# Cross-attention and FFN block on one core: x turned by VectorE in 32x32 pieces, its norm folded into q's, Wq loaded by row blocks

## What is computed

```python
x = x + xattn(layernorm(x), ctx, Wq, Wk, Wv, Wo, gq, bq, gk, bk)   # x: (2, 2048, 512), ctx: (2, 128, 512)
x = x + ffn(layernorm(x), Win, bin_, W1, b1, W2, b2, Wout, bout)

def xattn(h, ctx, ...):          # 16 heads of 32
    q, k, v = h @ Wq, ctx @ Wk, ctx @ Wv
    q, k = layernorm over the 32 of each head (q, gq, bq), (k, gk, bk)
    attn = softmax(q k^T / sqrt(32))
    return (attn v) @ Wo

def ffn(h, ...):
    s = h @ Win + bin_                                      # 64 columns
    g = (relu(s[..., None] * W1 + b1) * W2).sum(-1) + b2    # 16 units for each
    return g @ Wout + bout
```

## Time and profile before

| | |
|---|---|
| median of 3 runs | 443.71 us (442.64 to 443.96) |
| the profiled execution | 445.51 us, of which the span is 443.7 us |
| TensorE (PE) busy | 95% |
| VectorE (DVE) busy | 74% |
| ScalarE (ACT) busy | 71% |
| GpSimd (POOL) busy | 55% |
| packets on the DMA queue of SP, share of 16 engines | 50.5% |

### The profile page before, as it was taken

The page is one execution under the profiler, slowest core; times in us unless marked ns, Lnnn a source line. Parts: engine busy times, 40 slices in busy tenths (PEclk is TensorE's granted clock), DMA queues, the critical chain, the costliest instruction groups (busy, mean ns, idle before and its releaser), DMA issues.

```text
span 443.7 us, 7794 instructions
## 1 busy us (share of the span) xinstructions
PE 423.3 (95%) x2344; PEld 287.2 (65%) x2344; DVE 327.1 (74%) x652; ACT 315.3 (71%) x611; POOL 241.9 (55%) x326
## 2 busy tenths in 40 slices
PE   4999999999889999999999999999999999998994
PEld 2477887476557767576676757685665476556772
DVE  4888787746565999569874898479678985777765
ACT  5549768887487963899369974899559937953640
POOL 4419976586475484548156646165659036307084
PEclk9999999999999999999999999999999999999998
DMA  8662593965923339633493275705851980044005
GB/s 274 177 203 102 125 210 115 208 142 141 235 66 69 95 115 216 153 94 73 142 233 77 77 142 191 144 3 119 215 143 27 209 244 3 1 136 149 1 2 190
DMA packets 28106, 58.34 MB, mean 131 GB/s; under 512 B 8865, under 2 KB 9377, under 8 KB 24993
## 3 DMA queue, kind: packets, MB, share of 16 engines
q1 hardware_dynamic: 28064, 57.85, 50.5%
HBM read 22.18 MB, written 8.39 MB: 69 GB/s over the span
## 4 chain that ended last, share of the span: by engine, by line
PE 75%; DMA 7%; SPq 6%; POOL 3%; issue 3%; DVE 3%; ACT 1%; POOLq 1%; DVEq 0%; ACTq 0%
PE bank L2613 31%; PE bank L2619 9%; PE bank L2702 6%; PE bank L2690 6%; PE bank L2676 6%; PE bank L2705 4%; PE bank L2633 4%; PE bank L2755 3%; DMA out_dram<-x 3%; SPq L486 2%; SPq L433 2%; PE bank L2779 2%; DMA xin<-in_x_dram 2%; PE bank L2766 2%; DMA att<-in_L_xattn_Wk_dram 2%
## 5 line engine op out<-in xcount | busy, mean ns | idle before, releaser
L1074 DVE TENSOR_REDUCE mx<-bank 128x4 fp32r<-128x512 f32 x128 | 82.1, 684 | 21.9 <-PE bank L2676 21.5
L1854 ACT ACTIVATE prob<-bank 128x512 f32<-128x512 f32 x128 | 71.0, 609 | 16.6 <-PE bank L2690 10.7
L2702 PE MATMUL bank<-prob,v_kv 128*32 128x512 f32 x256 | 62.1, 599 | 0.0
L2705 PE MATMUL bank<-prob,den_sel 128*32 128x512 f32 x256 | 61.3, 599 | 0.0
L1935 ACT ACTIVATE hid<-s_in,b_col,w_col 128x256 f32<-128x256 f32 x105 | 56.8, 623 | 0.6 <-DVE s_in L1135 0.6
L2613 PE MATMUL bank<-wq_hi,zt_hi 128*128 128x512 f32 x128 | 51.5, 403 | 0.9 <-issue 0.9
L725 POOL TENSOR_TENSOR squares<-u 128x512 f32<-128x512 f32 x32 | 33.0, 1041 | 35.5 <-DVE ssq L1067 19.1
L737 POOL TENSOR_TENSOR qt_lo<-u,qt_hi 128x512 fp32r<-128x512 f32 x32 | 40.8, 1290 | 19.9 <-ACT qt_hi L1839 17.4
L2613 PE MATMUL bank<-wq_hi,zt_lo 128*128 128x512 f32 x128 | 50.6, 395 | 0.0
L2613 PE MATMUL bank<-wq_lo,zt_hi 128*128 128x512 f32 x128 | 50.6, 395 | 0.0
L1177 DVE SCALAR_TENSOR_TENSOR bank<-hid,w_col,bank 128x256 f32<-128x256 f32 x90 | 43.8, 487 | 5.1 <-ACT hid L1935 2.9
(11 more groups left out here) (175 smaller groups left out, 899.1 us busy)
## 6 DMA issues: line engine op xcount, KB each, us to landing
q_stack<-qt_hi SPq DMA_DIRECT2D x64, 256.0 KB, 4.7
...
```

The source lines that it names most:

```text
L1074: dve.tensor_reduce(mx[:, :].rearrange("p (g i j) -> p g i j", g=G, i=HC)[:, :, 2 * half + r, j], maxs_banks[T][half][j][r][:, :].rearrang ...
L1854: act.activation(prob[:, h % PR, :], score_bank[t][h][:, :], ACT.Exp, scale=SCALE).then_inc(exp_done, 1)
L2702: pe.matmul(at_bank[t][c][rows(n), :], v_kv[kv_of(t)][:, n * HD:(n + 1) * HD], prob[:, n % PR, :], start=True, stop=True)
L2705: ins = pe.matmul(den_bank[t][rows(n + 2), :], den_sel[:, c, :], prob[:, n % PR, :], start=c == 0, stop=c == C - 1)
```

## The change

**x.** It is loaded raw. load_x(T, half) brings two tiles with four DMAs of 32 partitions: partition group g gets columns 128 g to 128 g + 127 of x in pieces of 32 rows, so that a 32x32 transpose within partition groups (turn_x, VectorE, in place in xin) gives the turned tile. turn_z1 and z1_norm are gone, and z1_high reads xin. z1_low is done by VectorE for blocks 0 to 2 (z1_low_early) and by GpSimd from block 3 on. Since the rows that Wq meets are then in another order, Wq is loaded by four DMAs of 32 partitions in that order.

**The first norm.** Scaling a row of x by rstd scales q by it, and q is normed by head afterwards; so only the variance is needed, as an addition to q's sum of squares (add_eps: ssq + 32 eps var). The mean falls out if the columns of Wq sum to zero over the 512 inputs: sum_wq (TensorE, 4 fp32 matmuls of 128x512 against inv_d) and flatten_wq (VectorE, 4 of 128x512) take it out. The variance comes from a second load of each tile in its plain layout, xs (load_stats, 256 KB, 2 slots, stats1). guess1 and newton1 are gone.

**The start.** Wk comes in four loads, Wq ahead of x, and TensorE does 5 fp32 matmuls of 128x128 (spin) ahead of turn_ctx and 2 ahead of project_keys. wout_in and ctx_t move to other buffers; bout_row is loaded later.

All the written orders and bank tables are new. The core of the diff:

```diff
-            sp.dma_start(wk_in[:, :, :], Wk.rearrange("(c p) n -> p c n", p=P)).then_inc(wk_loaded, 16)
-            for j in range(TB):
-                sp.dma_start(xin[:, j, :], x_t[0, j]).then_inc(x_loaded[j], 16)
             for c in range(C):
-                sp.dma_start(wq_in[:, c, :], Wq[c * P:(c + 1) * P, :]).then_inc(wq_loaded[c], 16)
+                sp.dma_start(wk_in[:, c, :], Wk[c * P:(c + 1) * P, :]).then_inc(wk_loaded[c], 16)
+            wq_rows = Wq.rearrange("(q c e) n -> q e c n", q=G, c=C)
+            for g in range(G):
+                sp.dma_start(wq_in[HD * g:HD * (g + 1), :, :], wq_rows[g]).then_inc(wq_loaded[g], 16)
+            for half in range(2):
+                for g in range(G):
+                    sp.dma_start(x_parts[g][:, 2 * G * half:2 * G * (half + 1), :],
+                                 x_by_part[0, g][:, 2 * G * half:2 * G * (half + 1), :]).then_inc(x_loaded[g][half], 16)
...
-            def load_x(T, j):
+            def load_x(T, half):
 
-                sp.wait_ge(z1_turned, T * TB + j + 1 - TB)
-                sp.dma_start(xin[:, j, :], x_t[T, j]).then_inc(x_loaded[j], 16)
+                sp.wait_ge(zt_lo_done, T * TB - HT * (1 - half))
+                rows = slice(2 * G * half, 2 * G * (half + 1))
+                for g in range(G):
+                    sp.dma_start(x_parts[g][:, rows, :], x_by_part[T, g][:, rows, :]).then_inc(x_loaded[g][half], 16)
+
+            def load_stats(T, j):
+
+                if T * TB + j >= 2:
+                    sp.wait_ge(bn1_done, T * TB + j - 1)
+                sp.dma_start(xs[:, j % 2, :], x_t[T, j]).then_inc(xs_loaded[j], 16)
...
+            def z1_low(T, j):
+
+                if T == EARLY and j == 0:
+                    pool.wait_ge(zt_lo_done, EARLY * TB)
+                pool.wait_ge(zt_hi_done, T * TB + j + 1)
+                pool.tensor_tensor(zt_lo[:, j % 2, :, :].rearrange("p c (a s) -> p c a s", a=G), x_turned_of(j),
+                                   zt_hi[:, j % 2, :, :].rearrange("p c (a s) -> p c a s", a=G).bitcast(F32),
+                                   ALU.subtract).then_inc(zt_lo_done, 1)
...
+            def add_eps(T):
+
+                dve.wait_ge(mv1_done, T * TB + TB)
+                dve.wait_ge(ssq_done, T * TB + TB)
+                dve.scalar_tensor_tensor(out=ssq[:, :, :], in0=mv1[:, :, 1].unsqueeze(2).broadcast_to([P, TB, H]),
+                                         scalar=HD * EPS, in1=ssq[:, :, :], op0=ALU.mult, op1=ALU.add).then_inc(eps_added, 1)
+
+            def turn_x(T, j):
+
+                for g in range(G):
+                    dve.wait_ge(x_loaded[g][j // HT], T * 16 + 16)
+                dve.transpose(xin[:, j, :], xin[:, j, :]).then_inc(x_turned, 1)
...
+            def flatten_wq(c):
+
+                dve.wait_ge(wq_summed, 1)
+                dve.tensor_tensor(wq_in[:, c, :], wq_in[:, c, :], wq_mean_bank[:, :], ALU.subtract).then_inc(wq_flat, 1)
...
-            def z1_norm(T, j):
-                act.wait_ge(ln1_step, T * 7 + 7)
-                act.activation(xin[:, j, :], xin[:, j, :], ACT.Identity, bias=shift1[:, j:j + 1],
-                               scale=ln1[:, 3, j:j + 1]).then_inc(z1_done, 1)
...
+            def spin(dst, count):
+
+                for n in range(count):
+                    pe.matmul(dst[:, 0:P], inv_d[:, :], inv_d[:, :], start=True, stop=True)
...
-            def turn_z1(T, j):
-                pe.wait_ge(z1_done, T * TB + j + 1)
-                turn(z1_bank[T][j], columns(xin[:, j, :]), z1_turned)
+            def sum_wq():
+
+                pe.wait_ge(eyes, NEYES)
+                for c in range(C):
+                    pe.wait_ge(wq_centred, c + 1)
+                    ins = pe.matmul(wq_mean_bank[:, :], inv_d[:, :], wq_in[:, c, :], start=c == 0, stop=c == C - 1)
+                ins.then_inc(wq_summed, 1)
```

More of the change, by code:

```diff
@@ L27 @@
 LATE = 2
+EARLY = 3
 SUMMED = range(4, HH)
@@ L390, in _ @@
         def _(sp):
+            x_parts = [xin[HD * g:HD * (g + 1), :, :].rearrange("p j (a e) -> p (j a) e", e=P) for g in range(G)]
             column = lambda a: a.rearrange("(p o) -> p o", o=1)
@@ L437, in load_wout @@
             def load_wout():
-                for part in range(2):
-                    sp.wait_ge(kv_projected[part], NB)
+                sp.wait_ge(kv_projected[0], NB)
                 for half in range(2):
```

2636 lines of the change are left out of this document (1298 added, 1338 removed), and 32 rows, old and new, of tables (maxs_rows, score_bank).

## The result

The change made the kernel slower: 450.96 us median of 4 runs (449.72 to 452.18) against 443.83 of the kernel before (442.64 to 445.93), a ratio of 1.0157 with a 95% interval of 1.0113 to 1.0201. I had forecast 440.0. On another chip the changed kernel came out at 449.74 against 444.32, ratio 1.0136 (1.0097 to 1.0174).

A forecast was written before the change was run, and what follows sets the result against it. SP's loads at the start were taken as the bound: scores(0, 0) 6.0 us later, less 8.7 for turns and 0.9 for max_scores, gives -3.6, rounded to -3.7, from 443.7 to 440.0 us; range 430 to 447.

The forecast's parts named there:

- 9.6 us of TensorE's work behind scores(0, 0): After scores(0, 0), TensorE saves 8.7 us from 80 fewer turns and 0.9 us from two fewer pairs of max_scores.
- the bound of 1.4: VectorE's transpose of 128x512: upper bound of 1.4 us, from 8 times 0.17; 0.61 us was taken.
- the estimate of 1.24: VectorE's transposes for one tile: four of 128x128 at the Trainium skill's 311 ns, an estimated 1.24 us.
- the size of the start, +6.0: At the start, scores(0, 0) can't begin before 81.8 us, against 75.8 before: 6.0 us later, set by SP's loads.
- Nothing of this waits long: SP's loads up to stack_max(0) hardly wait: stack_q needs qt_lo, expected at about 55 us, before SP arrives at 57.4.
- stack_max(0) issued at 74.7: On SP: 57.4 us, then 13.6 for stack_q(0), then six more loads, reaching stack_max(0) at 74.7.
- rival 3: Part loads of x on SP cost 1.13 us each at worst, 14 us over 28, giving 454; chance 0.10.
- TensorE would be ready at 71: TensorE's work ahead of scores(0, 0) ends at 71 us, well inside SP's 81.8.
- TensorE's busy time down by some 12: Sign the forecast is right: over the whole kernel, TensorE's busy time falls by some 12 us.
- The 446.7: Forecast time if VectorE's transposes take the Trainium skill's figure, in place of 440.0; chance of slower by the transposes 0.09.
- TensorE idle for 8 us or more between 20 and 82: Sign the forecast is right, at the start: TensorE lacks work for at least 8 us between 20 and 82 us.
- SP's start bounds it: Likeliest case: SP's row of loads at the start sets the time, 437 to 442.4 us; chance 0.45.

The follow-up runs named there:

- wide parts: Changed kernel with each part load of x as 64 runs of 2 KB instead of 256 of 512 bytes (computes another function): 445.14 us, ratio 1.0036.
- x ahead: Changed kernel with block 1's x loads issued ahead of Wo and of stack_keys(0): ratio 1.0224 to the kernel before.
- three moves: Changed kernel with four of block 0's part loads later, block 1's x ahead of Wo and stack_keys(0), and wo_low behind q_low(1, 3): ratio 1.0169.
- Wo behind: Changed kernel with Wo's load issued behind block 1's first x loads and block 0's last xs: ratio 1.0128 to the kernel before.
- wo_low late: Changed kernel with GpSimd's wo_low moved behind q_low(1, 3): ratio 1.0190 to the kernel before.
- gap spins: Changed kernel with twelve spins added on TensorE ahead of project_q(1, 0): ratio 1.0192 to the kernel before.
- two moves: Changed kernel with block 0's last four part loads behind Wv and the keys' parameters, and wo_low behind q_low(1, 3): ratio 1.0098 to the kernel before.

## Why the prediction was wrong

**Right: what the change is worth in the middle.** 9.6 us of TensorE's work behind scores(0, 0), as worked out. So are the turns' pace of 0.109 us, the transposes at 0.59 to 0.63 us from start to start (mean duration 694 ns; the bound of 1.4 is out, and so is the estimate of 1.24 from the Trainium skill, whose row is for bf16), ScalarE's 24 us at no cost, GpSimd's z1_low from block 3 on at no cost (TensorE never waited for it). VectorE at 77% doesn't bind in the middle.

**Wrong: the size of the start, +6.0.** It came to +14.3, so the forecast had the sign wrong: 3.7 us faster, where the profiled span is 4.2 longer. The step that failed is "Nothing of this waits long: stack_q needs qt_lo, which I get at about 55". qt_lo(0) was done at 63.5, and stack_q(0) started with it, as it does in the kernel before (51.4). With the 13.6 us of stack_q(0) and six loads this alone puts "stack_max(0) issued at 74.7" at 81.6, and VectorE's turn_max(0), which I had at 74 and which came at 83.2, made it 83.5. By SP's row:

| term | predicted | measured | more |
|---|---|---|---|
| first 18 loads, head and other parameters | to 25.2 | to 27.7 | +2.5 |
| 52 loads ahead of stack_q(0) | 32.2 (0.62 each) | 34.5 (0.66 each) | +2.3 |
| wait for qt_lo(0), then stack_q(0) | 0 + 13.6 | 1.3 + 13.6 | +1.3 |
| six loads | 3.7 | 4.5 | +0.7 |
| wait for turn_max(0) on VectorE | 0 | 1.9 | +1.9 |
| stack_max(0) and its landing | 7.1 | 6.5 | -0.6 |
| scores(0, 0) | 81.8 | 89.9 | +8.1 |

The first row is the part loads: the eight took 0.82 us each and Wv behind them 1.54, where I had taken 0.57 from loads with 2 KB runs. The second is not: its 16 part loads took 0.61 each; the 12 loads of stack_keys(0) took 0.76 each, and SP waited 0.8 us ahead of load_stats(1, 2). So rival 3 (part loads dear on SP) came true for eight loads of 28. Nor do these two rows decide. Had SP come to stack_q(0) at 57.4 as forecast, it would have waited there until 63.5. Of the 8.1 us, 6.1 are qt_lo(0), 0.7 the six loads, 1.9 turn_max(0), and 0.6 come off.

Why qt_lo(0) was late: block 1's x is issued at 31.1 us, 0.4 behind VectorE's second zt_lo, ahead of which it may not go, and behind Wo's 1 MB and in runs of 512 bytes. It lands 8.3 us later, and VectorE, in its written order, holds the sums of block 0's q behind it. In the runs that brought the landing down to 5.0 us and less, wide parts, x ahead and three moves, qt_lo(0) was done at 59.9, 60.4 and 60.3; with Wo behind it was 62.2. That is a part of the 8.5 us. Another lies ahead of it: project_q(0) began at 30.0 us (23.5 before) and ended at 42.8, where I had 40. What the flatten and project_values(1) each have in that is not separated.

Why turn_max(0) came at 83.2 and not at 74, by my own terms: Wq arrived at 13.3 instead of 11 (2.3 us). The 78 operations of 512 columns, as many as I had counted, and the small ones kept VectorE busy for 62.6 us instead of 56.6 (6.0 us). Its waits were 7.3 us, where I had 7. So the size that was wrong is that of an operation beside GpSimd, for which I had taken the pace without it: add_eps(1) took 2.24 us (0.20 with wo_low out of the way), z1_low_early 922 ns on average against 682 from PSUM before, and fold_bias 3.7 in all. wo_low late gives 2.7 us back; how the rest divides was not tested.

Wide parts takes 3.5 us back at scores(0, 0) and about 1.2% of the time, the largest single step found, on another chip than the changed kernel.

I had also written that TensorE would be ready at 71. It wasn't, since it waits for VectorE's zt_lo; and "TensorE's busy time down by some 12" left out the spins: 14.0 less, with 3.6 for sum_wq and 3.7 for the spins as measured, gives 6.7, and the page shows 3.0. project_q has 1.4 of the rest, in part at the lower clock; what else is in it I did not trace. The 446.7 for the Trainium skill's transposes was a slip too: 12 x 0.63 less 0.7, on 440.0, is 446.9. TensorE idle for 8 us or more between 20 and 82 came true (10.6 between 20 and 80), but it waited for zt_lo, not for SP.

**The shape.** "SP's start bounds it" was right in kind: SP had no gap of over 1.4 us from 31 to 81.6, and where VectorE was brought forward most (77.8, 78.2) SP's row ended the wait at 82.3 and 79.05. But SP's row was itself started by qt_lo(0), and not by the number of loads ahead of it. At stack_max(0) SP and VectorE lie within 2 us of each other, with the arrival of x behind both, so that each edit gained a part of what it should and most gained less than the measurement can tell.

**Left open.** The medians differ by 5.4 and 7.1 us on the two chips, the profiled spans by 4.2. The profiled execution of the kernel before lies 1.7 us above the middle of its runs, that of the changed kernel 1.2 below: the whole difference of 2.9. Why single executions of one kernel differ by 2 to 3 us is not shown. The clock is not all of it: gap spins, with the highest mean clock of all (0.998), has a span of 449.3. x ahead was set against a median of 442.0 for the kernel before, which is a part of its high ratio; in microseconds it has 451.25, the changed kernel 450.96. For three moves (450.52 against 449.74 for the changed kernel in the same round) the difference is within the spread. No version found beats the kernel before; the best that computes the same is two moves, 448.17 us.
